# The order of the start of a graph network kernel: W first, a ring of 4 then 3 banks, and two units' products between the h W groups

## What is computed

```python
h = relu(layernorm(x))                     # (2048, 256)
ht = (h @ W).reshape(N, 4, 256)            # W is (256, 1024): 4 heads
src, dst = ht . a_src, ht . a_dst          # per head and node
e = leaky_relu(src[:, None] + dst[None, :], 0.01) + adj
x = x + mean over heads of softmax(e) @ ht
h = relu(layernorm(x))
x = x + ((adj != 0) @ (h @ W1 + b1)) / deg # deg = column sums of adj != 0
```

## Time and profile before

| | us |
|---|---|
| median of 3 runs | 596.38 |
| lowest, highest | 595.22, 596.96 |
| profiled execution, device time | 597.32 |
| its span in the trace | 595.5 |
| busy: TensorE, VectorE, ScalarE | 527.2, 455.1, 453.7 |
| hardware DMA queue q1, share of 16 engines' span | 85.1% |

### The profile page before, as it was taken

How to read it: one execution, slowest core, us unless ns; L and a number is a source line. 1 busy time by engine, 2 the same in 40 slices (tenths; PEclk the granted TensorE clock), 3 DMA queues, 4 the chain that set the end, 5 groups by cost and what they waited for, 6 DMA issues and landing times.

```text
span 595.5 us, 8989 instructions
## 1 busy us (share of the span) xinstructions
PE 527.2 (89%) x2992; PEld 308.9 (52%) x2992; DVE 455.1 (76%) x586; ACT 453.7 (76%) x379; POOL 33.2 (6%) x64
## 2 busy tenths in 40 slices
PE   7998889989797989798989899798989899687996
PEld 7843335545454545363545455454545455365885
DVE  6577968897786888687889798788888894455883
ACT  3377959998979697887898789979889892436660
POOL 3100000000000000000000000000000001001111
PEclk8799999999999999898999899999999999897999
DMA  8028518999999999999999999999999999741111
GB/s 307 3 100 273 106 36 183 223 219 212 225 196 226 194 200 210 212 185 234 201 233 220 210 236 198 228 209 229 204 231 216 216 203 185 212 141 63 45 44 35
DMA packets 300263, 108.76 MB, mean 183 GB/s; under 512 B 284720, under 2 KB 295360, under 8 KB 297680
## 3 DMA queue, kind: packets, MB, share of 16 engines
q1 hardware_dynamic: 300208, 108.45, 85.1%
q10 hardware_dynamic: 32, 0.01, 0.0%
HBM read 30.81 MB, written 6.32 MB: 62 GB/s over the span
## 4 chain that ended last, share of the span: by engine, by line
SPq 36%; PE 20%; DMA 12%; ACT 11%; DVE 10%; issue 10%; POOLq 0%; POOL 0%; DVEq 0%; ACTq 0%
SPq L305 15%; SPq L313 13%; DMA probs_hi_t<-probs_hi 9%; PE ps_relu L859 9%; PE ps_q L796 4%; ACT logits L548 3%; DVE probs_lo L1019 3%; ACT probs_hi L556 3%; SPq L323 2%; PE ps_q L772 2%; SPq L275 1%; DMA hidden_in<-hidden_scratch 1%; ACT ps_relu L540 1%; SPq L297 1%; DMA x<-in_x 1%
## 5 line engine op out<-in xcount | busy, mean ns | idle before, releaser
L796 PE MATMUL ps_q<-h_w_split,probs_hi_t 128*128 128x512 f16 x1024 | 250.9, 390 | 43.5 <-DMA probs_hi_t<-probs_hi 41.9
L796 PEld LDWEIGHTS ps_q<-h_w_split,probs_hi_t 128*128 128x128 f16 x1024 | 94.9, 100 | 162.2 <-issue 37.2
L540 ACT ACTIVATE ps_relu<-dst_rows,src_bias 128x2048 f32<-128x2048 f32 x63 | 124.0, 1968 | 56.9 <-DVE small L1010 56.7
L1010 DVE CUSTOM_DVE_ANT_0 logits<-ps_relu,adj_rows 128x2048 f32<-128x2048 f32 x48 | 110.0, 2291 | 46.8 <-PE ps_relu L782 44.9
L805 PE MATMUL ps_q<-h_w_split,probs_lo_t 128*128 128x256 f16 x1024 | 122.3, 273 | 0.7 <-DMA probs_lo_t<-probs_lo 0.6
L1019 DVE SCALAR_TENSOR_TENSOR probs_lo<-logits,small,probs_hi 128x2048 f16<-128x2048 f32 x48 | 112.7, 2349 | 6.0 <-ACT probs_hi L556 6.0
L805 PEld LDWEIGHTS ps_q<-h_w_split,probs_lo_t 128*128 128x128 f16 x1024 | 99.9, 98 | 25.5 <-DMA probs_lo_t<-probs_lo 2.7
L556 ACT ACTIVATE probs_hi<-logits,small 128x2048 f16<-128x2048 f32 x48 | 95.4, 1988 | 0.1
L548 ACT ACTIVATE logits<-logits,small 128x2048 f32<-128x2048 f32 x48 | 95.4, 1988 | 0.0
L859 PE MATMUL ps_relu<-hidden_split,mask_columns 128*128 128x512 f32 x256 | 62.8, 406 | 6.3 <-DVE hidden_split L1108 5.6
L859 PEld LDWEIGHTS ps_relu<-hidden_split,mask_columns 128*128 128x128 f32 x256 | 49.6, 195 | 18.2 <-DVE hidden_split L1108 6.3
(11 more groups left out here) (89 smaller groups left out, 322.5 us busy)
## 6 DMA issues: line engine op xcount, KB each, us to landing
adj_rows<-in_adj SPq DMA_DIRECT2D x16, 1024.0 KB, 6.3
dst_rows<-dst_scratch SPq DMA_DIRECT2D x4, 1024.0 KB, 5.6
x_all<-in_x SPq DMA_DIRECT2D x4, 512.0 KB, 6.8
x<-in_x SPq DMA_DIRECT2D x16, 128.0 KB, 2.5
x_scratch<-x SPq DMA_DIRECT2D x16, 128.0 KB, 2.0
hidden_scratch<-hidden SPq DMA_DIRECT2D x16, 128.0 KB, 2.2
out<-out_rows SPq DMA_DIRECT2D x16, 128.0 KB, 1.7
x_in<-x_scratch SPq DMA_DIRECT2D x1, 1792.0 KB, 8.3
```

The costliest lines, as they stand in the source:

```text
L540: nc.scalar.activation(R[:, :], rows, ACT.Relu, scale=(1.0 - SLOPE) / SLOPE, bias=src[:, bass.ds(u, 1)]).then_inc(relu_ready, 1)
L796: last = nc.tensor.matmul(ACC[parity][:, :], TA[:, e, b, :], H[:, h, b, :], start=(h == 0 and b == 0), stop=False)
L1010: nc.vector.tensor_tensor_reduce(out=logits_of(h, parity), in0=R[:, :], in1=ADJ[:, parity, :], scale=-1.0, scalar=3.0e38, op0=ALU.add, op1 ...
```

## The change

Six things are reordered; what is computed stays.

1. W is loaded ahead of x. The front's orders follow: TensorE turns W, makes the narrow products and the maximum, and only then turns h (three parts); the second keep_warm(6) is gone. ScalarE normalises part 2 instead of part 1.
2. weigh(0), (1) and (2) stand between and behind the scores.
3. Seeds 0 to 3 stand behind groups 6, 10, 14 and 18 instead of 5, 10, 15 and 20.
4. From group 17 on the groups use PW[1] to PW[3] alone, and from group 20 on weigh(g) waits for hw_low(g - 3).
5. Slot 0 stands behind group 21 and slot 1 behind group 26 on TensorE, ScalarE and VectorE; the other orders are fitted to it. On ScalarE `slot` is cut into `slot_high` and `slot_next`.
6. On VectorE `pieces` and the wait for b1 stand in the list of groups.

The calls with g, in the order of each engine, are the core of the diff:

```diff
+    def bank_of(g):
+
+        return PW[g % 4 if g < 17 else 1 + (g - 17) % 3]
...
-        load_x(0)
-        load_x(1)
         sp.dma_start(WR[:, :, :], w0.rearrange("(k p) d -> p k d", p=P)).then_inc(w0_in, 16)
-        load_x(2)
-        load_x(3)
+        for g in range(4):
+            load_x(g)
...
-        h_relu(1)
         w_columns(0)
         w_columns(1)
+        w_high(0)
         h_columns(0)
+        h_high(0)
+        h_relu(2)
         h_columns(1)
-        w_high(0)
-        h_high(0)
         h_columns(2)
+        h_high(1)
         h_columns(3)
-        h_high(1)
-        act.wait_ge(sd_summed, 1)
-        nc.scalar.activation(SD[:, :], DSP, ACT.Copy).then_inc(sd_ready, 1)
         h_high(2)
...
         h_high(3)
-        w_high(1)
...
+        def dst_rows():
+            act.wait_ge(sd_summed, 1)
+            nc.scalar.activation(SD[:, :], DSP, ACT.Copy).then_inc(sd_ready, 1)
...
+        def src_bias():
+            act.wait_ge(src_transposed, 1)
...
-        def slot(ib, h, parity):
+        def slot_high(ib, h, parity):
 
             u = 4 * ib + h
             if has(u + 2):
                 high(u + 2, 2 * ib + (h + 2) // 2, (h + 2) % 4, parity if h < 2 else 1 - parity)
+
+        def slot_next(ib, h, parity):
+
...
-        for g in range(3):
-            hw_high(g)
-        relu_term(0, 0)
-        for g in range(3, 8):
-            hw_high(g)
-        relu_term(1, 1)
-        hw_high(8)
-        exp(0, 0, 0)
...
-        high(0, 0, 0, 0)
-        for g in range(15, 18):
-            hw_high(g)
-        relu_term(3, 3)
-        hw_high(18)
-        exp(2, 2, 0)
...
-        relu_term(4, 0)
-        hw_high(23)
-        exp(3, 3, 0)
-        for g in range(24, GROUPS):
-            hw_high(g)
+        def prefix():
+            hw_high(0)
+            hw_high(1)
+            dst_rows()
+            w_high(1)
+            hw_high(2)
+            src_bias()
+            hw_high(3)
+            hw_high(4)
+            relu_term(0, 0)
...
+            relu_term(2, 2)
+            hw_high(13)
+            high(0, 0, 0, 0)
+            hw_high(14)
+            exp(1, 1, 0)
+            hw_high(15)
+            hw_high(16)
+            relu_term(3, 3)
+            hw_high(17)
+            high(1, 0, 1, 0)
+            hw_high(18)
+            exp(2, 2, 0)
+            hw_high(19)
+            hw_high(20)
+            relu_term(4, 0)
+            hw_high(21)
+            exp(3, 3, 0)
+            slot_high(0, 0, 0)
+            hw_high(22)
+            hw_high(23)
+            slot_next(0, 0, 0)
+            for g in range(24, 27):
+                hw_high(g)
+            slot_high(0, 1, 0)
+            slot_next(0, 1, 0)
+            for g in range(27, GROUPS):
+                hw_high(g)
 
         def body(ib, parity):
-            for h in range(HEADS):
-                slot(ib, h, parity)
+            if isinstance(ib, int) and ib == 0:
+                prefix()
+            for h in range(2 if isinstance(ib, int) and ib == 0 else 0, HEADS):
+                slot_high(ib, h, parity)
+                slot_next(ib, h, parity)
         block_loop(act, body)
...
-        turn_h(0)
...
-        pe.wait_ge(a_ready, 1)
-        turn_h(1)
...
+        pe.wait_ge(a_ready, 1)
...
-        keep_warm(6)
+        turn_h(0)
+        turn_h(1)
         turn_h(2)
-        pe.wait_ge(wa_ready, 1)
-        scores(0)
-        scores(1)
-        turn_h(3)
-        scores(2)
-        scores(3)
...
+            if g <= 2:
+                pe.wait_ge(ht_ready, 3 if g < 2 else 4)
...
             if g >= 4:
-                pe.wait_ge(hw_lo_ready, g - 3)
+                pe.wait_ge(hw_lo_ready, g - 3 if g < 20 else g - 2)
...
-        for g in range(GROUPS):
-            weigh(g)
-            if g == 0:
-                src_columns()
-            if g == 2:
-                spread_dst0()
-            if g % 5 == 0 and 1 <= g // 5 <= 4:
-                seed(g // 5 - 1, g // 5 - 1)
-        pe.wait_ge(hw_lo_ready, GROUPS)
-        pe.wait_ge(w1_in, 16)
+        def prefix():
+            weigh(0)
+            pe.wait_ge(wa_ready, 1)
+            scores(0)
+            scores(1)
+            turn_h(3)
+            weigh(1)
+            scores(2)
+            scores(3)
+            weigh(2)
+            src_columns()
+            weigh(3)
+            weigh(4)
+            spread_dst0()
+            for g in range(5, 22):
+                weigh(g)
+                if 6 <= g <= 18 and g % 4 == 2:
+                    seed((g - 6) // 4, (g - 6) // 4)
+            pe.wait_ge(hw_lo_ready, NB + 1)
+            slot(0, 0, 0)
+            for g in range(22, 27):
+                weigh(g)
+            slot(0, 1, 0)
+            for g in range(27, GROUPS):
+                weigh(g)
+            pe.wait_ge(hw_lo_ready, GROUPS)
+            pe.wait_ge(w1_in, 16)
 
         def body(ib, parity):
-            for h in range(HEADS):
+            if isinstance(ib, int) and ib == 0:
+                prefix()
+            for h in range(2 if isinstance(ib, int) and ib == 0 else 0, HEADS):
                 slot(ib, h, parity)
         block_loop(pe, body)
...
-        x_stats(0)
-        x_stats(1)
-        x_norm(0)
-        x_bias(1)
         vec.wait_ge(w0_in, 16)
         nc.vector.tensor_reduce(WM[:, 0:1], WR[:, :, :], AX0.XY, ALU.max, apply_absolute_value=True)\
...
-        x_stats(2)
+        x_stats(0)
...
-        x_stats(3)
-        x_norm(2)
+        x_stats(1)
+        x_norm(0)
         vec.wait_ge(w_max_spread, 1)
...
         nc.vector.tensor_scalar(w_scale[:, :], MAXB[:, 1:2], W_SCALE, None, ALU.mult).then_inc(w_scale_ready, 1)
+        x_stats(2)
+        x_norm(1)
+        x_bias(2)
+        w_low(0)
+        h_low(0)
+        x_stats(3)
...
         x_norm(3)
-        w_low(0)
-        h_low(0)
         h_low(1)
-        pieces()
-        vec.wait_ge(b1_in, 16)
...
-        hw_low(0)
-        h_low(2)
-        hw_low(1)
-        h_low(3)
-        hw_low(2)
-        w_low(1)
-        hw_low(3)
-        mask_rows(0, 0)
-        hw_low(4)
-        logits(0, 0, 0, 0)
...
+        def prefix():
+            hw_low(0)
+            hw_low(1)
+            pieces()
+            hw_low(2)
+            h_low(2)
+            w_low(1)
+            hw_low(3)
+            hw_low(4)
+            h_low(3)
+            hw_low(5)
+            mask_rows(0, 0)
+            vec.wait_ge(b1_in, 16)
+            hw_low(6)
+            logits(0, 0, 0, 0)
+            for g in range(7, 11):
+                hw_low(g)
...
+                hw_low(g)
+            logits(2, 0, 2, 0)
+            hw_low(15)
+            low(0, 0, 0, 0)
+            hw_low(16)
+            row_inverse(1, 1)
+            hw_low(17)
+            hw_low(18)
+            logits(3, 0, 3, 0)
+            hw_low(19)
+            low(1, 0, 1, 0)
+            hw_low(20)
+            row_inverse(2, 2)
+            hw_low(21)
+            slot(0, 0, 0)
+            for g in range(22, 27):
+                hw_low(g)
+            slot(0, 1, 0)
+            for g in range(27, GROUPS):
+                hw_low(g)
 
         def body(ib, parity):
-            for h in range(HEADS):
+            if isinstance(ib, int) and ib == 0:
+                prefix()
+            for h in range(2 if isinstance(ib, int) and ib == 0 else 0, HEADS):
                 slot(ib, h, parity)
         block_loop(vec, body)
```

More of the change, by code:

```diff
@@ L523, in hw_high @@
                 nc.scalar.activation(H[:, 2 * pair:2 * pair + 2, b, 0:F],
-                                     PW[g % 4][:, :].rearrange("p (h f) -> p h f", h=2),
+                                     bank_of(g).rearrange("p (h f) -> p h f", h=2),
                                      ACT.Copy, scale=HT_SCALE).then_inc(hw_hi_ready, 1)
@@ L568, in slot @@
                     high(u + 2, 2 * ib + (h + 2) // 2, (h + 2) % 4, parity if h < 2 else 1 - parity)
+            def slot_next(ib, h, parity):
+                u = 4 * ib + h
                 if h == 0 and past(ib, 2):
@@ L606, in hidden_high @@
                                      ACT.Copy).then_inc(hid_hi_ready, 1)
-            for g in range(3):
-                hw_high(g)
-            relu_term(0, 0)
-            for g in range(3, 8):
-                hw_high(g)
-            relu_term(1, 1)
-            hw_high(8)
-            exp(0, 0, 0)
-            for g in range(9, 13):
-                hw_high(g)
-            relu_term(2, 2)
-            hw_high(13)
-            exp(1, 1, 0)
-            hw_high(14)
-            high(0, 0, 0, 0)
@@ L623, in _ @@
-            for g in range(15, 18):
-                hw_high(g)
-            relu_term(3, 3)
-            hw_high(18)
-            exp(2, 2, 0)
-            hw_high(19)
-            high(1, 0, 1, 0)
-            for g in range(20, 23):
-                hw_high(g)
-            relu_term(4, 0)
-            hw_high(23)
-            exp(3, 3, 0)
-            for g in range(24, GROUPS):
-                hw_high(g)
-            def body(ib, parity):
```

(58 more changed lines are left out.)

11 lines of the change are left out of this document (4 added, 7 removed).

## The result

The changed kernel took 600.01 us (median of 20 runs, 595.81 to 602.66) against 597.16 us of the kernel before in 20 runs: a ratio of 1.0044, 95% interval 1.0024 to 1.0063. It is 0.44% slower, where 594.1 and a ratio of about 0.996 were forecast.

A forecast was written before the change was run, and what follows sets the result against it. The prediction took the kernel's middle to hang on DMA transfers, crowded from 101.3 us on. Its terms, +0.9 + 0.4 - 3.6 = -2.3 us, applied to the median 596.38, gave 594.1 us, range 589.5 to 600.

The forecast's parts named there:

- The front: Up to the first logits: W loaded first, logits(0) starting at 45.7 against 44.82 us, +0.9 us.
- Some 2.5 to 3.5 us more of it: At weigh(0): TensorE at half clock when it starts and for this much longer, +1.5 us.
- The price formula: For TensorE's half clock after weigh(0) starts: half-speed time costs half its length, taken as +1.5 us.
- From logits(0) to unit 2: The middle stretch, with two units' products among the groups: 51.7 us against 51.3 before, +0.4 us.
- My chain: Logits(0) to unit 2, counted with listed durations: 51.7 us, with 42 us of ScalarE work and about 6.7 of waits.
- The rejected rule: Groups on cycling banks: a Trainium skill page says short waits can make the clock swing; the forecast added 0.
- The 8 us: Estimated cost of half clock for half of the 32 us from 65 to 97, left out of the sum.
- Behind unit 2: Unit 2 to unit 8: earlier transfers avoid the crowded queue, unit 8 at +35.6 instead of +39.2, -3.6 us, kept afterwards.
- (3): Middle: ScalarE runs of about 6 us stall the three-bank ring; three stalls make 600 us; chance 0.17.
- (4): TensorE at half clock for half of 65 to 97 us, costing 8 us, time 602; chance 0.03.
- (1): TensorE without holes from weigh(0) on, unit 2 starting 5 us earlier, time near 589.5 us; chance 0.15.
- (2): Later blocks' high transposes stay late, the -3.6 shrinks to about -1, time 596.5 to 597 us; chance 0.15.

The follow-up runs named there:

- warm_front: The changed kernel with 3, 6 and 4 warm-up products behind turn_h(0), (1) and (2); ratio 1.0003 against the kernel before.
- old_front: The kernel before's front with the changed kernel's list from group 3 on (seeds, interleaved slots, three banks); ratio 1.0012 against the kernel before.
- all_three: The changed kernel with warm-up products between the turns, the maximum's spread ahead of the narrow products, and later seeds; ratio 0.9979 against the kernel before.
- ring_only: The kernel before with only banks 1 to 3 from group 17 on and the wait for hw_low(g - 3) from group 20; ratio 1.0041.
- interleave_only: The kernel before with three banks from group 17 on and slots 0 and 1 behind groups 22 and 27; ratio 1.0000.
- max_first_warm: The changed kernel with warm-up products between the turns and the maximum's spread ahead of the 32 narrow products; ratio 0.9999 against the kernel before.
- before_cold: The kernel before with only the line keep_warm(6) taken out; ratio 0.9979.

## Why the prediction was wrong

**It said faster, and it is slower**, for which it had a chance of 0.23, and 600.01 lies just above the range. Most of the mechanism was right; three terms of the sum were mis-sized, all in the same direction: half clock in the front, the way from logits(0) to unit 2, where a wait of over 2 us and the clock behind it were put at nothing, and the transpose at unit 8.

1. *The front, +0.9, measured +2.65.* W's landing (5.2 us after an issue at 0.73, so 5.9), the W turns at full clock, the serial chain through x_stats(2), the bias, the relu and three turns, and half clock at weigh(0) were all as written. "Some 2.5 to 3.5 us more of it" was the wrong sentence: half clock lasted 4.3 us from the start of weigh(0), and it had covered the turns too, 1.97 us each where I took 0.9 to 1.3. So weigh(0) began at 23.75 and not at 22.7, and from there to the end of the scores it took 12.6 us and not 11.9. The price formula held: 1.2 us in weigh(0) and 0.9 in the scores, 0.9 in the last turn. warm_front gives the term by itself: 2.5 us. The forecast priced the half clock from the kernel before, where it ended behind a dense stretch, and not for turns with holes between them.

2. *From logits(0) to unit 2, +0.4, measured +2.45.* My chain ran through ScalarE and VectorE here, and TensorE's wait for relu(1) stood in it at nothing; 2.49 us of wait came, and the clock fell behind it for 3.4 us: 1.25 us, the difference of the changed kernel to old_front. The other 0.8 are small waits that a chain with means doesn't have: 52.53 in old_front and all_three against my 51.7. In old_front the chain holds to 0.2 us up to the end of unit 1's products (43.3 against 43.1), and the rest comes in the last five groups, with 1.00 us of wait ahead of weigh(30). The rejected rule was the right one in kind. The Trainium skill's page "TensorE: Matmul & The Clock Gate", section "A second HAM failure mode: psum-queue depth-cycling", describes a clock that swings when the engine idles between groups on cycling banks. I set it aside since the trace of before showed 1.00 with 6.9 us of waits (5.5 of them for a bank); but none of those was over 1.42 us, and in the runs above a fall follows single waits of 1.9 to 2.5 us, most of the time. It agrees with the traces as to the kind: in ring_only the wait was for a bank, in the changed kernel for relu(1). The 8 us were an estimate of mine and not the page's, and far too much: one stretch of 3.4 us came, for 1.25. The trace of before had such a wait too, in its front, and I passed it over:

```profile
9.65 1.26 PE L687 MATMUL ps_q<-ident,x_all 128*128 128x128 f32 x8 [2.46 <-DVE x_all L916]
```

The clock fell 0.8 us behind it, to the 0.51 of the second row.

3. *Behind unit 2, -3.6, measured -2.3.* The mechanism held point by point: adj(2) at 96.2 us, hi(4) landing in 4.2 us, unit 4 11.3 us behind unit 2, the shift kept to unit 60 within 0.2. The size failed at hi(8): issued 28.8 us behind unit 2 and not 28.1, landed after 8.0 and not 7.3. The shares of the queue ahead of it are not a constant.

Of the rivals, (3) named three banks as the way to slower, and ring_only shows that three banks can cost 0.41%; but in the changed kernel the waits for hw_low are 2.7 us in all, fewer than before, and the largest wait is for relu(1). I had it on ScalarE's runs of 6 us; no bank is waited for behind the first of them, and behind the second come 1.00 us ahead of weigh(30) and 1.42 ahead of unit 2. (4) came in small. (1) and (2) didn't come. One sum of the middle was off without moving the forecast: 51.7 less 42 us of ScalarE's work leaves 9.7 us of waits and not 6.7, and the changed kernel has 9.8.

What stays open: the ratio and the marks up to unit 8 don't always move alike. By the marks unit 8 stands 2.2 us later than before in interleave_only and 3.2 in max_first_warm, where the ratio shows nothing, and 3.4 earlier in before_cold, where it shows 1.3. The scatter of 4.7 us from unit 8 to unit 60 is large enough for that, but no run here tells chance of the profile from an effect on the blocks behind. What in the new list costs 1.2 us up to unit 2 isn't shown either.

## What to carry to other kernels

When a change takes dense work out of TensorE's queue or puts waits in it, price the clock at each place where the new order waits about 2 us or longer, and price it from rows at either level: the same products cost nearly twice as much behind it (weigh(0) 2.74 us instead of 1.46), and the price falls on whatever stands there. A smaller ring of banks is to be checked against the longest single instruction ahead of its release on each engine, not against the average. And a rule of thumb that a trace seems to refute is refuted only for the waits that this trace has, its front included. Try the smallest edit by itself first: one line less gave as much here as the best of the new orders.
